# Attention on TensorE: third head group's transposes placed behind the next tile's scores

## What is computed

```
x = x + 0.5 * moe(layernorm(x))
x = x + attention(layernorm(x))          # the change is here
x = x + 0.5 * moe(layernorm(x))
x = x + 0.5 * ternary_ffn(layernorm(x))
x = x + selective_scan_block(layernorm(x))
x = x + 0.5 * ternary_ffn(layernorm(x))
```

```
qkv = x @ w_qkv.T ; scores = q @ k.T / sqrt(8)
allowed = (j <= i) & (i - j < 64)
attn = softmax(where(allowed, scores, -inf))
out = (attn @ v) @ w_out.T + b_out
```

## Time and profile before

| | us |
|---|---|
| median of three runs | 540.64 |
| lowest and highest run | 540.5 and 543.88 |
| the profiled execution | 541.29 |
| its span on the core | 539.6 |
| attention: first scores to the last tile's last values | 45.0 to 183.1 |

### The profile page before, as it was taken

The page is one execution under the profiler, slowest core; times in us unless marked ns, Lnnn a source line. Parts: engine busy times, 40 slices in busy tenths (PEclk is TensorE's granted clock), DMA queues, the critical chain, the costliest instruction groups (busy, mean ns, idle before and its releaser), DMA issues.

```text
span 539.6 us, 10085 instructions
## 1 busy us (share of the span) xinstructions
PE 474.9 (88%) x3844; PEld 287.2 (53%) x3844; DVE 442.3 (82%) x892; ACT 267.8 (50%) x414; POOL 300.9 (56%) x225
## 2 busy tenths in 40 slices
PE   7998999989899989999687798789879777889996
PEld 3876767777677767677231243233323232337674
DVE  4678878878589476758978999999999999998753
ACT  2345646565555525656786546446443434330743
POOL 3348030030200012467415889999999999993581
PEclk9999999999999989999986789889989998989998
DMA  7000000000000000000009934444454354200002
GB/s 219 7 0 22 4 2 24 2 21 3 4 23 4 1 0 2 1 1 2 0 19 391 383 133 184 155 156 190 200 233 155 156 206 164 97 0 1 2 22 58
DMA packets 14402, 43.84 MB, mean 81 GB/s; under 512 B 3017, under 2 KB 10834, under 8 KB 12306
## 3 DMA queue, kind: packets, MB, share of 16 engines
q1 hardware_dynamic: 13538, 42.67, 21.0%
q10 hardware_dynamic: 816, 0.53, 0.3%
HBM read 40.78 MB, written 1.31 MB: 78 GB/s over the span
## 4 chain that ended last, share of the span: by engine, by line
PE 43%; DVE 23%; issue 15%; POOL 10%; ACT 7%; POOLq 0%; DVEq 0%; ACTq 0%
DVE hst L1078 9%; PE bk L460 6%; PE bk L466 6%; PE bk L748 5%; PE bk L1224 5%; PE bk L733 4%; POOL hC L1154 4%; PE bk L719 3%; DVE xnT L280 3%; DVE dBu L1057 3%; PE bk L705 3%; ACT bk L1313 2%; POOL powers L294 2%; ACT g L874 2%; ACT g L868 2%
## 5 line engine op out<-in xcount | busy, mean ns | idle before, releaser
L1154 POOL TENSOR_TENSOR hC<-hst,rows 128x1024 f32<-128x1024 f32 x62 | 144.3, 2349 | 13.1 <-DVE hst L1078 10.6
L1078 DVE TENSOR_TENSOR_SCAN hst<-bk,dBu 128x1024 f32<-128x1024 f32 x64 | 144.8, 2278 | 2.7 <-POOL dBu L1138 2.5
L1224 PE MATMUL bk<-hC,ident 128*128 128x512 f32 x256 | 129.5, 641 | 1.3 <-ACT ysb L1303 1.0
L1313 ACT ACTIVATE bk<-delta,aneg 128x1024 f32<-128x1024 f32 x64 | 71.5, 1118 | 97.5 <-DVE hst L1078 97.4
L1224 PEld LDWEIGHTS bk<-hC,ident 128*128 128x128 f32 x256 | 51.8, 205 | 54.5 <-issue 44.7
L287 POOL TENSOR_TENSOR veps<-mv,lneps 128x4 f32<-128x4 f32 x24 | 5.7, 238 | 124.3 <-DVE mv L259 124.2
L541 ACT ACTIVATE rows<-bk 128x512 f32<-128x512 f32 x64 | 37.7, 591 | 58.6 <-PE bk L460 58.6
L1204 PE MATMUL bk<-s,sel 96*128 96x512 bf16 x100 | 33.5, 420 | 31.4 <-DVE dBu L1057 28.5
L1057 DVE TENSOR_TENSOR dBu<-bk,du 128x1024 f32<-128x1024 f32 x50 | 60.1, 1202 | 0.8 <-PE bk L1204 0.8
L874 ACT COPY g<-bk 128x512 f32<-128x512 f32 x64 | 37.8, 590 | 23.5 <-PE bk L733 23.5
L598 DVE TENSOR_REDUCE smax<-bk 128x4 f32<-128x512 f32 x64 | 43.6, 681 | 5.9 <-PE bk L719 5.9
(11 more groups left out here) (176 smaller groups left out, 766.9 us busy)
## 6 DMA issues: line engine op xcount, KB each, us to landing
rows<-c_rows SPq DMA_DIRECT2D x16, 2048.0 KB, 7.1
rows<-c_rows SPq DMA_DIRECT2D x4, 1024.0 KB, 10.3
x<-in_x_dram SPq DMA_DIRECT2D x4, 256.0 KB, 4.8
out_dram<-x SPq DMA_DIRECT2D x4, 256.0 KB, 2.3
rows<-rows SPq DMA_DIRECT2D x4, 144.0 KB, 2.5
wmoe<-in_w_dram ACTq DMA_DIRECT2D x2, 256.0 KB, 4.9
rows<-rows SPq DMA_DIRECT2D x4, 108.0 KB, 2.3
wup<-in_upT_dram SPq DMA_DIRECT2D x1, 256.0 KB
```

The source lines that it names most:

```text
L1078: nc.vector.tensor_tensor_scan(hst[k % 3][:, :], dA[k % 2][:, :], dBu[k % 3][:, :], 0.0, ALU.mult, ALU.add).then_inc(m2["scan"], 1)
L1154: nc.gpsimd.tensor_tensor(hC[k % 4][:, :], hst[k % 3][:, :], crep[:, k % 12, :], ALU.mult).then_inc(m2["hC"], 1)
L1224: last = nc.tensor.matmul(bk01[:, r * CH:(r + 1) * CH], ident[:, :], hC[k % 4][:, r * CH:(r + 1) * CH], start=(k % NS == 0), stop=(k % NS ...
L1313: nc.scalar.activation(dA[k % 2][:, :], delta[:, i, :], ACT.Exp, scale=aneg[:, h * NS + n:h * NS + n + 1]).then_inc(m2["dA"], 1)
```

## The change

The call `prob_t(t, 2)`, the four transposes of the third head group, is moved on PE only. For t = 0 to 14 it stood between `context_t(t-1)` and `project(t-1)`, ahead of `scores(t+1)`; now it stands behind `scores(t+1)` and the `mask_behind(t+1, 1)` that `scores` issues at its end, ahead of `values(t, 0)`. In the last tile (t = 15), which has no next scores, it stays. No instruction is added or removed, and no wait of any instruction changes.

```
@@ -796,11 +796,13 @@
                     expert_up(0)
                 if t > 0:
                     context_t(t - 1)
-                prob_t(t, 2)
+                if t == NT - 1:
+                    prob_t(t, 2)
                 if t > 0:
                     project(t - 1)
                 if t + 1 < NT:
                     scores(t + 1)
+                    prob_t(t, 2)
                 if t == NT - 2:
                     expert_transposes()
                 if t == NT - 1:
```

## The result

The changed kernel takes 544.6 us, the median of 22 runs (541.58 to 550.06), against 540.61 for the kernel before, also of 22. The ratio of the comparable runs is **1.0046, with a 95% interval of 1.0026 to 1.0066**: slower by 1.4 to 3.6 us. The ratio is that of the means, 543.99 to 541.48 us; one slow run of the changed kernel, the 550.06, is left out of it. The forecast was +1.7 us with 542.3 as the time, no change within 1%, and a range from 539.4 to 545.4. The mechanism and the sign came out; one term was mis-sized, and where the clock fell was not foreseen.

A forecast was written before the change was run, and what follows sets the result against it. PE was taken as the bound, 88% busy, with DVE close behind. 15 insertions at 0.43 us (6.45) less 14 gains of 0.34 (4.76) gave +1.7 on 540.64, so 542.3 us; range 539.4 to 545.4 for 8 in 10.

The forecast's parts named there:

- What PE meets next: On PE ahead of the scores: the projection waits for ACT's context copy, 0.55 us in ordinary tiles, 1.08 with the key projection.
- The cost of the insertion: Four transposes moved between mask and values on PE: 0.43 us a tile, 15 times, 6.45 us in all.
- the fourth group's row: Fourth group's transposes between mask and values: 0.75 us from mask to values, against 0.32 without transposes; taken as the insertion's price.
- neither 0.32 nor 0.66: Bounds on the insertion's cost per tile: 0.32 us for weight loads only, 0.66 as transposes held the scores back in tile 0.
- The gain: Scores on PE start earlier, at 85.76 in place of 86.10 in tile 4: 0.34 us, 14 times, 4.76 us.
- The cross-check "+0.09 a tile": PE per tile: wait grows 0.15 us, transposes cost 0.06 less in a stream than behind a wait, so +0.09.
- The forecast's own case: Whole kernel: net +1.7 us, 542.3 us, range 540.8 to 544.3; chance 0.62.
- the not-overlapped rival: Moved transposes on PE cost the full 0.66 us at their new place: +5.1 us, 545.8 us; chance 0.10.
- The clock rival: PE's clock falls in three attention tiles as the gap grows to 1.08 us: 5.1 us more, 547.4 us; chance 0.06.
- the 1.39 gap: PE's gap before an up-projection, which then took 5.38 us against 3.68 early on, at granted clock 0.50: 1.70 us lost.
- DVE's gate, POOL and SP: DVE's fourth subtraction does not bind the scores; POOL's queries and SP's value transfers shift with PE and cost nothing.

## Why the prediction was right, and where it was off

**What PE meets next: right.** The projection waits for the context copy (0.56 us in ordinary tiles, forecast 0.55; 1.08 in the key-projection tile, forecast 1.08), and the copy waits behind the exponential:

```profile
114.14 0.27 ACT L882 COPY cxT<-bk 128x128 f32<-128x128 f32 x1
114.46 0.49 PE L778 MATMUL bk<-wproj,cxT 128*128 128x128 f32 x2 [1.08 <-ACT cxT L882]
```

The swap of the two on ACT shows this: it takes 0.21 off an ordinary tile with the projection first, and adds 0.48 with the transposes first.

**The cost of the insertion: right.** 0.44 in the kernel with only tile 0 moved, 0.44 in tile 4 (mask to values 0.76 for 0.32). Taking the fourth group's row as the price, kind and neighbours being the same, was sound; neither 0.32 nor 0.66 came true.

**The gain: mis-sized, 0.24 for 0.34.** The failed step is "the scores follow a projection after 86.10 - 85.78 = 0.32". That row is of a projection which ran straight behind other matmuls. There its weight load begins at 85.67, 0.11 ahead of its matmul at 85.78, and from load to load (scores at 86.09) it is 0.42:

```profile
85.67 0.30 PEld L778 LDWEIGHTS bk<-wproj,cxT 128*128 128x128 f32 x2
86.09 0.97 PEld L719 LDWEIGHTS bk<-delta,rows 32*64 32x64 f32 x64
```

In the changed kernel the projection has waited, its load and its matmul begin together (88.07 and 88.08), and the scores' load comes again 0.42 later. It is so in all 14 tiles of both traces: 0.31 to 0.32 from matmul to matmul where the load ran 0.10 to 0.11 ahead, 0.41 to 0.42 where it did not, and 0.41 to 0.43 from load to load in both. So ahead of scores the spacing goes by the loads, and the head start of one load is lost in a wait. Why the loads are 0.42 apart is not shown, and the rule is no wider than this pair. In tile 15 the load has no head start either, but an up-projection follows in place of scores, with its load 0.22 and its matmul 178.58 - 178.25 = 0.33 later:

```profile
178.25 0.30 PEld L778 LDWEIGHTS bk<-wproj,cxT 128*128 128x128 f32 x2 [0.16 <-ACT cxT L880]
178.47 0.30 PEld L460 LDWEIGHTS bk<-xnT,wmoe 128*128 128x128 f32 x2
```

From that row I took only the 0.05; the load without a head start was the sign that I passed over. The cross-check "+0.09 a tile" missed the same thing: it gave the transposes 0.06 back for leaving a wait, and charged the projection nothing for coming into one. So the ordinary window is 7.87 and not 7.75, the one with the key projection 10.17 and not 10.06.

**The sum with the measured term.** 15 x 0.43 - 14 x 0.24 = +3.1 us, in place of +1.7. The traces agree. The cleanest stretch is from scores 1 to the up-projection that follows PE's 1.39 us gap, in executions without a fall in it. In the trace of before it is 191.63 - 51.71 = 139.92 us, and 139.92 and 139.91 in the two others. In the last two executions of the changed kernel it is 143.02 each, so 3.10 more; one of them:

```profile
51.82 1.21 PE L719 MATMUL bk<-delta,rows 32*64 32x128 f32 x64 [1.11 <-DVE g L603]
194.84 3.68 PE L460 MATMUL bk<-xnT,wmoe 128*128 128x512 f32 x8
```

In the first profile of the changed kernel the up-projection begins at 196.30, 4.67 later than in the one of before. Of this 0.11 is there from the start of the attention (scores 0 at 45.13 for 45.02, scores 1 at 51.82 for 51.71) and 9.35 - 7.87 = 1.48 is the fall of the clock, which leaves 3.08. Over all runs about the same comes out: with time fitted as a line over each run's mean clock, the changed kernel has 544.2 us at 0.954 (21 runs) and the kernel before 540.8 (17 runs, taken beside the experiments), 3.4 apart, and both lose about 0.39 us for each 0.001 of clock. The ratio gives 2.5, with 3.1 inside its interval.

**Some of the fit is luck.** The forecast's own case reached only to 544.3, and the median, 544.6, is above it. It lies inside the range to 545.4 because the range was drawn up into the not-overlapped rival, which did not come true: the insertion cost 0.44 and not 0.66.

**The clock rival: a fall came, but not where or as I gave it.** I had put the deciding point between gaps of 0.93 and 1.39 us and priced three falls, one in each key-projection tile. None came there. One came in tile 0, behind a wait of the scores of 1.11 us that the prediction had not listed (with no projection and no transposes ahead of them, the scores of tile 1 wait for DVE alone). PE's rows there are at half speed:

```profile
51.82 1.83 PE L719 MATMUL bk<-delta,rows 32*64 32x128 f32 x64 [1.11 <-DVE g L603]
53.59 0.61 PE L705 MATMUL bk<-rows,identb 128*128 128x512 bf16 x1
```
```profile
52.00:53.00 1.00, 1.00 (x53) 1.00 (x53) 1.00 (x3) 0.43 (x1) 0.71 (x1) 0.55 0.08 16
53.00:54.00 1.00, 1.00 (x28) 0.47 (x15) 0.85 (x4) 0.00 (x0) 0.29 (x1) 0.50 0.00 0
```

But in these runs no length of gap decides. The 1.11 was followed by a fall in one execution of the changed kernel and by none in the other three. And the 1.39 gap, which I took as the proof, was followed by one in 6 of the 14 profiles, 2 of 3 with the kernel before. In the changed kernel's first profile it was not:

```profile
195.41 1.03 PE L485 MATMUL bk<-wg,xnT 128*128 128x8 f32 x8 [1.39 <-issue]
196.30 3.68 PE L460 MATMUL bk<-xnT,wmoe 128*128 128x512 f32 x8
```

So the 1.48 us that tile 0 lost were about given back by the 1.70 that were not lost here, and the two spans differ by 3.4, near the 3.1 of the work itself. What the Trainium skill says of transposes (TensorE: Matmul & The Clock Gate, "PE-mode transpose") was not put to the test by any run: no kernel changed how many there are.

**DVE's gate, POOL and SP: right.** In the changed kernel L603 releases no scores beyond tile 0, and windows with queries or value transfers grew by the same 0.20 as the others.

## What to carry to other kernels

Before work is moved out of a wait, look who releases what comes next: if that is queued on the same engine behind the same instruction, the wait only changes its name, and the moved work is paid for where it lands. The better place to mend was the engine that releases: in tile 4 ACT had the data of the third exponential from 82.40 + 0.69 = 83.09 on and began it at 84.60, with other exponentials, a copy and 0.27 us of idleness between, and a different order there took 5 us off. A start-to-start distance read where an engine runs in a stream need not hold behind a wait.

```profile
82.40 0.69 DVE L603 TENSOR_TENSOR g<-bk,smax 128x512 f32<-128x512 f32 x1
```

## What was not expected of the hardware

- The projection's distance to the scores behind it is 0.32 us in a stream and 0.41 to 0.42 behind a wait; from weight load to weight load it is 0.42 in both. With an up-projection behind it, it is 0.33 although its load had no head start.
- The same program with the same gaps lets the clock fall in different places: the window from scores 1 to scores 2 took 9.35, 7.87, 7.86 and 7.86 us in four executions of the changed kernel, and the up-projection at 10 us took 5.38 us in one of them and 3.68 in the kernel before, behind the same gap of 0.68. In one execution the clock fell at 128 us, where PE's rows show no wait after that of the projection, 6 us earlier. One fall costs 1.2 us (9.03 for 7.87) to 2.6 (19.35 for 16.78 in two windows), so a sum of less than 2 us is not to be read off one pair of spans, but off windows in which the clock is 1.00.
